# A second store queue in the message stage of a three-layer graph kernel: ScalarE issues the stores of the even groups, one group late

## What is computed

```python
msg = vals[:, None] * x[col]
h = jax.ops.segment_sum(msg, row, num_segments=N)
z = (h + x_prev) @ W_a.T + b_a + h * x_prev @ W_b.T + b_b
x_next = jnp.where(z >= 0, z, 0.2 * z)
```

## Time and profile before

| what | value |
|---|---|
| median of three runs | 9937.94 us (9937.42 to 9949.97) |
| the profiled execution's own time | 9886.18 us |
| its span, first to last instruction | 9884.4 us |
| TensorE busy | 8882.5 us (90%) |
| VectorE busy | 8003.4 us (81%) |
| ScalarE busy | 4360.8 us (44%) |
| granted TensorE clock, mean | 0.922 |
| DMA, hardware queue of SyncE | 934.49 MB |
| DMA, software queue of GpSimd | 958.17 MB |

### The profile page before, as it was taken

How to read it: one execution, slowest core, us unless ns; L and a number is a source line. 1 busy time by engine, 2 the same in 40 slices (tenths; PEclk the granted TensorE clock), 3 DMA queues, 4 the chain that set the end, 5 groups by cost and what they waited for, 6 DMA issues and landing times.

```text
span 9884.4 us, 225675 instructions
## 1 busy us (share of the span) xinstructions
PE 8882.5 (90%) x69832; PEld 8123.9 (82%) x69833; DVE 8003.4 (81%) x11536; ACT 4360.8 (44%) x13665; POOL 4932.1 (50%) x2699
## 2 busy tenths in 40 slices
PE   6488888778888849999999999999999999999999
PEld 4366666456667639998999999989999999999999
DVE  7599999699999977777777777777777777777777
ACT  0377777047777715663111155651111465521112
POOL 8477777047777700004888700018888200068885
PEclk8688888878888859999999999999999999999999
DMA  2111111011111199999888879998888699988886
GB/s 71 40 6 6 6 6 6 15 10 6 6 6 6 6 36 340 345 340 303 282 285 285 266 256 342 344 324 283 285 285 284 220 342 337 333 289 285 285 284 209
DMA packets 1101073, 1893.75 MB, mean 192 GB/s; under 512 B 388436, under 2 KB 439704, under 8 KB 1100344
## 3 DMA queue, kind: packets, MB, share of 16 engines
q0 software_dynamic: 378656, 958.17, 32.7%
q1 hardware_dynamic: 722328, 934.49, 31.9%
HBM read 1136.46 MB, written 755.66 MB: 191 GB/s over the span
## 4 chain that ended last, share of the span: by engine, by line
PE 44%; DVE 23%; DMA 16%; issue 10%; ACT 3%; DVEq 1%; SPq 1%; POOL 0%; another core or an unknown queue 0%; ACTq 0%; POOLq 0%
PE ps L906 32%; DMA messages<-work 15%; PE ps L897 7%; DVE hT L1093 7%; DVE place L1072 7%; DVE hT L1087 4%; ACT work L670 3%; PE ps L746 1%; DVE hT L1220 1%; PE ps L914 1%; PE ps L934 1%; PE ps L935 1%; DVE place L1077 0%; DVE place L1075 0%; DVE work L1053 0%
## 5 line engine op out<-in xcount | busy, mean ns | idle before, releaser
L511 POOL DMA_INDIRECT work<-messages,work x1776 | 2722.6, 1533 | 3577.3 <-issue 3575.9
L906 PE MATMUL ps<-work 128*128 128x125 f32 x28416 | 3295.3, 278 | 41.7 <-DVE work L1273 37.8
L906 PEld LDWEIGHTS ps<-work 128*128 128x128 f32 x28416 | 3242.2, 192 | 94.8 <-DVE work L1273 62.5
L897 PE MATMUL ps<-xb,work 125*128 x21504 | 2457.9, 277 | 181.0 <-DVE work L1245 119.0
L897 PEld LDWEIGHTS ps<-xb,work 125*128 125x128 f32 x21504 | 2423.9, 193 | 214.9 <-issue 214.0
L486 POOL DMA_INDIRECT sorted_edges<-stage,run_idx x798 | 1969.9, 2469 | 1232.0 <-ACT stage L615 509.0
L1273 DVE TENSOR_TENSOR work<-work,iota_p 128x1000 f32<-128x1000 f32 x1776 | 2120.2, 1194 | 34.6 <-ACT work L688 34.2
L670 ACT ACTIVATE work<-ps,work 128x128 f32<-128x128 f32 x5376 | 1508.2, 372 | 1210.5 <-DMA messages<-work 665.5
L793 PEld LDWEIGHTS ps<-hT 128*128 128x128 f32 x12768 | 1694.9, 216 | 69.8 <-issue 47.3
L688 ACT ACTIVATE work<-work 128x8 f32<-128x8 f32 x1776 | 534.4, 301 | 2686.3 <-DMA work<-messages,work 2686.3
L626 ACT ACTIVATE hT<-iota_p,place 128x128 f32<-128x128 f32 x4788 | 1427.9, 387 | 652.2 <-DVE place L1077 645.7
(11 more groups left out here) (203 smaller groups left out, 3650.1 us busy)
## 6 DMA issues: line engine op xcount, KB each, us to landing
messages<-work SPq DMA_DIRECT2D x2688, 256.0 KB, 6.2
work<-slot_cols SPq DMA_DIRECT2D x672, 256.0 KB, 6.0
work<-messages,work POOLq DMA_INDIRECT x1776, 5.9
out_x<-xb SPq DMA_DIRECT2D x150, 125.0 KB
sorted_edges<-stage,run_idx POOLq DMA_INDIRECT x798, 3.7
work<-lane_places SPq DMA_DIRECT2D x532, 5.2 KB
out_x<-xb SPq DMA_DIRECT2D x4, 1562.5 KB
sorted_edges<-hT SPq DMA_DIRECT2D x4, 908.0 KB
```

Of the source, the lines that this page charges most:

```text
L511: pool.indirect_dma_start(out=ck[:, n, :, :].rearrange("p h x -> p (h x)"), out_offset=None, in_=flat, in_offset=bass.IndirectOffsetOnAxis ...
L897: last = t.matmul(ps[:, n % PR, j * D:(j + 1) * D], col_hot[:, n % OHR, j * P:(j + 1) * P], x_flat[:, bass.ds(offs[n], D)], start=True, st ...
L906: last = t.matmul(part[n], ck[:, n, j // CH, j % CH * D:(j % CH + 1) * D], sel[:, n % SELB, j, :], start=j == 0, stop=j == CHB - 1)
```

## The change

ScalarE gets a function that stores an even message, and calls it for group n - 2 after it has kept group n, and once more at the end of the body. SyncE's loop keeps the odd groups and the loads of column numbers. Semaphores, buffers and all arithmetic stay.

```diff
                 def store_messages(i, last):
-                    for n in range(AU):
-                        sp.wait_ge(msg_ready[n % 2], la * (GROUPS // 2) + i * (AU // 2) + (ACREDIT + n // 2 + 1))
+                    for n in range(1, AU, 2):
+                        sp.wait_ge(msg_ready[1], la * (GROUPS // 2) + i * (AU // 2) + (ACREDIT + n // 2 + 1))
                         sp.dma_start(messages[bass.ds(i * (AU * P) + n * P, P), 0:CH * D], msg[:, n % MR, :]).then_inc(msg_stored[n % MR], DMA)
...
+                def store_even(i, n):
+                    act.wait_ge(msg_ready[0], la * (GROUPS // 2) + i * (AU // 2) + (ACREDIT + n // 2 + 1))
+                    act.dma_start(messages[bass.ds(i * (AU * P) + n * P, P), 0:CH * D], msg[:, n % MR, :]).then_inc(msg_stored[n % MR], DMA)
+
                 def keep_messages(i, first):
...
                         last.then_inc(msg_ready[0], 1)
+                        if n >= 2:
+                            store_even(i, n - 2)
+                    store_even(i, AU - 2)
```

## The result

The changed kernel takes 10008.42 us (median of 4 runs, 10002.61 to 10016.30) against 9937.97 us for the kernel before, run beside it. The ratio is 1.0069, with a 95% interval of 1.0051 to 1.0086: **slower**, where faster was forecast. The profiled execution took 10004.18 us, its span is 10002.4 us. So the two traces show where the stage changed; how much it costs is taken from runs on one chip, further down.

What follows compares the result with a forecast made beforehand. The prediction took DMA throughput, felt through eight buffers, as the bound. Its only nonzero term, -41 us for two queues, gave 9845 us against the profiled execution's 9886.2, or 9897 applied to the median 9937.9; range 9860 to 9918.

Steps and rivals of the forecast that it cites:

- What bounds the kernel now: Message stages: DMA throughput sets the pace, felt through eight message buffers; TensorE, with at most 0.40 us a body, just behind.
- The even store comes a pair late: ScalarE's queue: three even stores under way, not four; landing shrinks from 6.2 to 3.2 us, limit 4.2; cost 0.
- The DMA engines serve two queues: DMA engines in the message stages: parting stores from loads wins back 1.6% of 2596 us, 41 us.
- the 4%: DMA engines' time said to be lost because stores and column loads in one queue stand in each other's way; 104 us.
- ScalarE's issues: ScalarE gets 8 store issues a body, 1344 in all, at 0.41 us each; it has room, so cost 0.
- SyncE's stores: SyncE loses half its stores; its queue is not full, so fewer issues gain nothing: 0.
- the low end of the range: 9860 us: TensorE's limit of 9871, with 11 us for a register load that may itself get faster.
- three even stores under way: Slower rival: late even stores bind from a landing of 4.2 us; at 4.4 us, 85 us more, 10023; chance 0.15.
- No change: Rival: the same DMA engines move the same bytes at the same rate, 9938 us; chance 0.28.
- the signs named in advance: Slower rival's marks: ScalarE's landing wait above 216.6 us, even landing over 4.2, mid-body TensorE pauses, DMA share under 1.04.
- high end of 10020: Upper end named for the time in us, where the slower rival stands at an even landing of 4.4 us.

Runs made afterwards that it cites:

- h1: The kernel before, with TensorE's register load split into eight block numbers at a time, read in mid-body half a body ahead: ratio 0.9999 to before, 9955.53 us.
- h3: The changed kernel with even stores issued before the buffer wait and the register load half a body early: ratio 1.0014 to before, 9978.13 us.
- b0: The kernel before, unchanged, run again on the chip of the third group of runs: ratio 1.0000, 9963.10 us.
- e3: The kernel before, with the column loads moved to ScalarE's queue and all stores kept on SyncE: ratio 1.0132 to before, 10003.29 us.
- e1b: e1 run again on the chip of the last group of runs: ratio 1.0025 to before, 9985.57 us.
- e1: The changed kernel, with ScalarE storing message n - 2 ahead of its wait for the buffer of message n: ratio 1.0068 to before, 9949.79 us.
- h3b: h3 run again on the chip of the last group of runs: ratio 1.0009 to before, 9965.10 us.

## Why the prediction was wrong

**What bounds the kernel now: right, as far as h1 shows it.** DMA throughput, felt through the eight buffers, with TensorE just behind.

**The even store comes a pair late: here it failed.** The step said "I expect it to: ... 2.4 + 0.8 = 3.2 us", on the idea that the engines take the two queues in turn. Measured: 5.7 us, about the same as in the other queue. The Trainium skill ("DMA: Bandwidth & Descriptors", section "Queues, rings and completion order") says that each engine takes turns at packets between queues. That may hold for packets, but it did not make the lighter queue's transfers land sooner (5.7 against 5.5 us). The landing shrank only as the number under way does. Five transfers take two pairs, 4.0 us, so one takes 0.80 us, and a landing of 5.6 us (between 5.5 and 5.7) means 7.0 under way where there were 8.1: one store fewer, shared by both queues. The limit in the same step was also off, to the other side: 3 x 1.92 - 1.55 = 4.2 us counted the keeping and the issue, while ScalarE's queue issues the store beside the activations, so that only 0.37 us counts and the limit is 3 x 1.92 - 0.37 = 5.4 us. 5.7 lies just over it, by (5.7 + 0.37) / 3 - 1.92 = 0.10 us a pair, or some 139 us. Taken alone it cost 71, since without it a pair took 1.99 us and not 1.92 on that chip.

**The DMA engines serve two queues: failed.** The gain of 41 us from parting stores and loads is 0: 1.04/334 in h3 against 1.04/332 in b0, and 1.03/340 in e3, where all loads are parted from all stores, against 1.04/340 before. The three stretches in the earlier trace rows from which the 4% came are 1.5 to 3 us long, from the start and the drain of a stage, and were no measure of the mixture.

**ScalarE's issues: right,** 338 + 46 + 29 ns are the 0.41 us, and they run beside the activations. **SyncE's stores: right,** no gain, though SyncE no longer waits for ScalarE (147.7 us before).

**A term put at nothing:** the register load of TensorE as something that gets longer. The sum has no term for it, and only the low end of the range lets it get faster, by 11 us. Its median went from 1.6 or 1.7 us to 2.0 in the changed kernel and 1.9 in e1b.

**The rivals.** The slower one, "three even stores under way", is what happened, by its own mechanism; it had a chance of 0.15 and a price of 85 us. That the price is near the measured 70 is luck: it took a landing of 4.4 us and a limit of 4.2, where 5.7 and 5.4 are measured. At 5.7 us its own formula, (5.7 + 1.55) / 3, gives 2.42 us a pair, a loss of some 670 us. "No change" would have needed that the lateness be hidden. Of the signs named in advance, the rival's came: ScalarE's wait on landings grew, an even landing over 4.2 us, pauses of TensorE in mid-body released by ScalarE, a share under 1.04. The measured 10008 lies outside the forecast's own 9860 to 9918 us, below the high end of 10020, on the side that was not forecast.

## What to carry to other kernels

Before a store is moved to the engine that fills the buffer, write down its loop: landing of the old store, wait, issue. Count it over a whole loop body, with what the end of the body does differently. A store placed behind the wait for the next buffer takes one buffer out of the ring, and where transfers queue, the landing is set by all of them, not by the queue that issues. If a second queue is wanted, issue ahead of the wait (e1, which still lost 0.25 to 0.7% here); and where the DMA engines are full, expect nothing from it.

## What was not expected of the hardware

- Two hardware queues with loads of 3 : 2 gave nearly equal landings (5.5 and 5.7 us in the changed kernel, 5.8 and 6.1 in h3) and, in h3, the same rate as one (334 GB/s, 332 in b0).
- A register load of 16 values on TensorE's queue takes 1.1 us at least, and in the median 1.6 to 2.2 us in the runs at 320 to 340 GB/s. In the traces of before and after the next weight load starts at least 0.46 us after its end, so none of the next body's begins while it runs. Of 8 values, in h3b at line 902, it takes half of that:

```profile
L902 PEldq TENSOR_LOAD <-work x168: 588/877/1922, 3724.8 to 8757.8; - x168
```

- 128 pieces of 4 bytes beside a stream of stores cost 2.2 us a transfer, three times what a transfer of 256 KB takes here (0.77 us), and in the trace most of that shows as longer packets of the other transfers.
- The same kernel ran at 9887 to 9963 us on different chips, 0.8% apart, as much as the effect under study.
